# A decoder layer on one core: TensorE's program written out for all heads, the softmax sums in groups 9 and 1, and another order on VectorE and in the transfer queue

## What is computed

```python
def attn(h, Wq, Wk, Wv, Wo, rel_bias):         # 16 heads of 64, S = 2048, two batches
    q, k, v = (proj(W) for W in (Wq, Wk, Wv))   # B,H,S,64
    scores = einsum('bhqd,bhkd->bhqk', q, k) + bias(rel_bias)   # by bucket of the distance
    a = softmax(scores, axis=-1)
    return merge_heads(einsum('bhqk,bhkd->bhqd', a, v)) @ Wo.T
x = x + attn(layernorm(x))
x = x + cross_attn(layernorm(x), ctx)           # 77 keys
x = x + ffn(layernorm(x))                       # a light FFN, and a heavy one for 512 routed rows
```

## Time and profile before

| | us |
|---|---|
| median of 3 runs (lowest, highest) | 3972.28 (3969.41, 3975.57) |
| the profiled execution | 3972.34 |
| its span, from the first to the last instruction | 3970.6 |
| busy in the span: PE, DVE, ACT, POOL | 3727.9, 2466.4, 2004.6, 2681.1 |

### The profile page before, as it was taken

One profiled execution on the slowest core, in us unless ns is written; L12 is line 12 of the kernel. 1 busy time (PEld: TensorE's weight loads), 2 busy tenths in 40 slices (PEclk: granted clock), 3 DMA queues, 4 the chain that ended last, 5 costly groups with the idle time before them and its releaser, 6 DMA issues. The chain is left out here.

```text
span 3970.6 us, 64135 instructions
## 1 busy us (share of the span) xinstructions
PE 3727.9 (94%) x21277; PEld 2216.2 (56%) x21277; DVE 2466.4 (62%) x3356; ACT 2004.6 (50%) x3452; POOL 2681.1 (68%) x1402
## 2 busy tenths in 40 slices
PE   8989999999999989999999999999997999997899
PEld 7754444444444444444444444444446888885377
DVE  3466666666666656666666666666635777775632
ACT  3335555555555555555555555555553555553232
POOL 1128888888888878888988888889893343430010
PEclk9989999999999999999999999999998999998999
DMA  7652222432223452222332222332312333335710
GB/s 221 162 120 63 66 64 71 103 75 69 64 64 81 101 153 64 69 64 67 93 90 66 68 64 67 98 84 65 105 36 88 100 106 103 104 116 174 262 46 22
DMA packets 368370, 366.99 MB, mean 92 GB/s; under 512 B 189339, under 2 KB 261531, under 8 KB 362776
## 3 DMA queue, kind: packets, MB, share of 16 engines
q1 hardware_dynamic: 299064, 336.50, 31.6%
q10 hardware_dynamic: 67168, 20.98, 2.2%
q0 software_dynamic: 1920, 6.29, 0.5%
HBM read 142.64 MB, written 89.70 MB: 59 GB/s over the span
## 5 line engine op out<-in xcount | busy, mean ns | idle before, releaser
L354 POOL TENSOR_TENSOR acc<-acc,probs 128x1024 f32<-128x1024 f32 x894 | 2126.4, 2379 | 306.9 <-ACT probs L814 189.3
L939 DVE TENSOR_REDUCE maxes<-ps 128x2 f32<-128x1024 f32 x1024 | 1253.2, 1225 | 607.6 <-PE ps L610 596.7
L817 ACT ACTIVATE probs<-ps,far_bias 128x1024 f32<-128x1024 f32 (+7 forms) x1280 | 997.4, 819 | 795.4 <-DVE near_s L956 546.0
L641 PE MATMUL ps<-probs,v_head 128*64 128x512 f32 x4096 | 1002.1, 610 | 8.9 <-ACT ctx_out L800 6.9
L629 PE MATMUL ps<-stacks 64*128 64x512 f32 x6144 | 825.7, 398 | 1.8 <-ACT probs L814 1.8
L629 PEld LDWEIGHTS ps<-stacks 64*128 64x128 f32 x6144 | 591.0, 188 | 126.9 <-ACT probs L814 7.9
L610 PE MATMUL ps<-stacks 64*128 64x512 f32 x2048 | 508.0, 494 | 142.4 <-DVE maxes L939 56.9
L610 PEld LDWEIGHTS ps<-stacks 64*128 64x128 f32 x2048 | 194.5, 187 | 700.0 <-DVE maxes L939 464.3
L641 PEld LDWEIGHTS ps<-probs,v_head 128*64 128x64 f32 x4096 | 251.0, 137 | 463.0 <-issue 450.9
L956 DVE TENSOR_TENSOR near_s<-ps,near_bias 128x384 f32<-128x384 f32 (+2 forms) x576 | 265.8, 491 | 58.4 <-PE ps L629 55.3
L962 DVE TENSOR_TENSOR c_q<-ps,c_q 64x512 fp32r<-64x512 f32 x128 | 87.5, 684 | 311.2 <-ACT c_q L773 311.2
(11 more groups left out here) (278 smaller groups left out, 4515.4 us busy)
## 6 DMA issues: line engine op xcount, KB each, us to landing
stacks<-c_q SPq DMA_DIRECT2D x128, 256.0 KB, 4.3
stacks<-c_d SPq DMA_DIRECT2D x64, 512.0 KB, 6.9
stacks<-c_k SPq DMA_DIRECT2D x32, 768.0 KB, 5.5
stacks<-c_k SPq DMA_DIRECT2D x64, 384.0 KB, 7.0
scr_v<-probs ACTq DMA_DIRECT2D x32, 512.0 KB, 4.1
v_head<-scr_v SPq DMA_DIRECT2D x32, 512.0 KB, 8.5
scr_ctx<-ctx_out SPq DMA_DIRECT2D x128, 128.0 KB, 2.3
both_ctx<-scr_ctx SPq DMA_DIRECT2D x32, 512.0 KB, 4.0
```

The lines of the kernel that those rows point to most:

```text
L354: pool.tensor_tensor(acc[:, qb, :], acc[:, qb, :], pr, ALU.add).then_inc(s["summed"], 1)
L641: mm = pe.matmul(ps[64 * half:64 * half + 64, PV, :], v_head[:, side, kt, :], probs[:, st % PT_RING, half * 512:(half + 1) * 512], start=k ...
L817: ins = act.activation(probs[:, st % PT_RING, a:z], sc[:, a:z], ACT.Exp, bias=bias)
L939: dve.tensor_reduce(maxes[:, qt:qt + HALF_GROUPS // 2 + 1:HALF_GROUPS // 2, first_chunk + pair], ps[:, bank:bank + 2, :], AX.X, ALU.max).t ...
```

## The change

TensorE's heads are written out by a Python loop over all heads; the other engines keep their loops. `sum_of` moves from groups 13 and 5 to groups 9 and 1, the reciprocals from 14 and 6 to 10 and 4, and `context` from ahead of steps 31 and 15 to ahead of steps 25 and 13. `project` waits for the sums' copies one quarter earlier, as their groups ask for. On SP `divisors` is cut in two: `spread` issues the four small transfers, `divisors` does the rest. For the second half `spread` stands right behind `fill`; for the first half both stand ahead of the `guard` of the next head. On VectorE the second `largest` of a group stands ahead of `step` and `step_lo`.

```diff
-SUM_GROUPS = {13: 0, 5: 1}
-RECIP_GROUPS = {14: 0, 6: 1}
-CONTEXT_STEPS = {31: 0, 15: 1}
+SUM_GROUPS = {9: 0, 1: 1}
+RECIP_GROUPS = {10: 0, 4: 1}
+CONTEXT_STEPS = {25: 0, 13: 1}
...
-            def divisors(n, qb):
+            def spread(n, qb):
 
                 sp.wait_ge(s["sum_out"], 2 * n + qb + 1)
                 for q in range(QUARTERS):
                     sp.dma_start(part[QP * q:QP * q + QP, :],
                                  sums[QP * q:QP * q + 1, 0:QUARTER].rearrange("o (p c) -> o p c", c=PART)).then_inc(s["spread"], 16)
+
+            def divisors(n, qb):
+
                 sp.wait_ge(s["recip"], 2 * n + qb + 1)
...
                 if nxt:
                     fill(n + 1, 1 - side)
+                if carry:
+                    spread(n - 1, 1)
                 if nxt and not early:
...
                     xn_block(1, reload)
+                if own:
+                    spread(n, 0)
+                    divisors(n, 0)
                 if nxt:
                     guard(n + 1, 1 - side, 0)
...
                 if own:
-                    divisors(n, 0)
                     store_ctx(n, 0)
...
-                    if tb == 1:
+                    if tb == 0:
                         past(pe, s["sum_out"], 2 * (m - 2))
-                    if tb == 3:
+                    if tb == 2:
                         past(pe, s["sum_out"], 2 * (m - 2) + 1)
...
-            heads(pe, head)
+            for n in range(-2, NH):
+                head(n, n // 2, n % 2)
...
+                    if has_max(n, g):
+                        largest(n, side, g, 1)
                     if prep and g in STEP_GROUPS:
                         step(n + 2, STEP_GROUPS[g])
                     if lowered:
                         step_lo(*lowered)
-                    if has_max(n, g):
-                        largest(n, side, g, 1)
```

## The result

| | before | changed |
|---|---|---|
| median, us | 3972.61 (4 runs) | 3796.56 (4 runs, 3794.21 to 3800.00) |
| ratio, 95% interval | 1 | 0.9558 (0.9541 to 0.9574) |
| profiled execution, its span | 3972.34, 3970.6 | 3797.64, 3795.8 |

The kernel became faster by 176 us. The forecast was 3818.6, with 3804 to 3872 as the range. The direction and the mechanism held, but the time lies 22 us under the forecast and 7.4 us under the whole range.

What follows compares the result with a forecast made beforehand. TensorE was taken to set the pace, busy in 95% of 85.07 us a head. Losses of 159.2 us, less 7.3 and 2.6 kept, plus 4.4, gave 153.7 off 3972.3: 3818.6 us, range 3804 to 3872.

Steps and rivals of the forecast that it cites:

- VectorE's order: Groups 11, 12, 15, 0 and 3: maximum first recovers losses of 2.35 us a head, except 0.25 us left.
- floor of a head from the group lengths: Heads 1 to 29: 79.58 us a head if TensorE never waited, added up from undisturbed groups.
- VectorE's residual: Next maximum slightly late in groups with two wide near: 0.25 us a head kept, bounds 0 and 0.7.
- the head of the reload (14): Where normalized rows are reloaded ahead of the fill, the longest wait, 11.8 us, keeps about 2.6 us, once.
- heads 30 and 31: The tail without project, where GpSimd is busy nearly throughout: nothing but 4 us to gain.
- The loop: TensorE's branch: 1.5 us lost in each of 13 pairs of heads, then slow clock; straight code costed at nothing.
- The stacks: Group 3: moving the store lets fill start 7 us earlier, so the wait and slow clock behind it go.
- branch's loss and this wait are one: Group 15's branch and group 3's stacks wait: removing the branch alone lengthens the wait; with slow clock, 3.14 us a head.
- The spread's place: SP's second-half spread behind fill costs nothing; fill ends in group 1, reciprocals over 10 us later.
- The rule that the prediction weighed against the place: Queue transfers go in ring order, so four of 1 KB behind the stacks' would wait for the fill's rest.
- the slower rival: Groups 4 and 10: VectorE waits for spread sums, 4.6 us each, giving 4085; chance 0.09, of which 0.06 slower.
- GpSimd: Last addition fits before the sum in group 9 by 2 to 3 us; as bound, 3867, chance 0.19 with fetch.

Runs made afterwards that it cites:

- D: The change's VectorE part: the group's second maximum ahead of step and step_lo; alone on the kernel before, 3944.86 us.
- e6: The changed kernel with VectorE's old order, step and step_lo ahead of the group's second maximum; 3870.37 us.
- e12: The kernel before with TensorE written out, 102 idle waits a head, and 154 more instructions once ahead, moving the fetch behind the stacks' transfers; 3999.40 us.
- U: The change's TensorE part: heads written out instead of looped; alone on the kernel before, 4003.84 us.
- S: The change's part with the sums' groups, context's steps, project's waits and SP's order; alone on the kernel before, 3892.59 us.
- e5: The changed kernel with TensorE's program left as a loop over two heads; 3827.66 us.
- e11: The kernel before with TensorE written out and 102 idle waits a head, so each head's fetch falls among the stacks' transfers; 4082.58 us.
- e1: The kernel before with TensorE's heads written out and nothing else; 4003.84 us, ratio 1.0090.
- e2: The kernel before with VectorE's other order and nothing else; 3944.86 us, ratio 0.9932.
- e4: The changed kernel with the sums' groups, context's steps and SP's order put back; 3976.55 us, ratio 1.0015.
- e8: The changed kernel with SP's spread and divisors of the first half put back behind the next head's guard; 4082.33 us, ratio 1.0278.
- e7: The changed kernel with SP's spread of the second half put back to where its divisors stand; 3934.57 us, ratio 0.9899.
- e9: The changed kernel with two more weight-sized subtractions on GpSimd in every head from 0 to 29; 3847.50 us, ratio 0.9691.

## Where the prediction held, and the step that failed

The mechanism held, and the sum failed: it had 153.7 us, and 174.8 were measured. The steps that failed are one of its terms and two stretches that it left out. VectorE's order was left 0.25 us a head, 7.3 us, where the heads keep nothing. What stands ahead of head 1 was put at nothing in the sum, and 7.5 us were gained there. What stands behind the heads was put at nothing too, and the profile of the change is 5.8 us shorter there, for a cause that stays open. The range's low end, 3804, had already taken off the 7.3 and 2.6 us and some 5 us "of the heads ahead". So what put the time outside the range is the 5.8 us behind the heads and 3 more ahead of them, less 2 that heads 30 and 31 gained less than forecast.

| step | forecast, us | measured, us |
|---|---|---|
| floor of a head from the group lengths | 79.58 | 79.53 |
| VectorE's residual, 29 heads | 7.3 kept | 0 |
| the head of the reload (14) | 2.6 kept | 0.7 kept |
| a fetch among the stacks' transfers (head 2) | not seen | 0.9 kept |
| heads 1 to 29 together | 149.3 gained | 159.3 |
| ahead of head 0, and head 0 | nothing in the sum | 3.8 and 3.7 gained |
| heads 30 and 31 | 4.4 gained | 2.2 |
| behind the heads | nothing | 5.8 gained |
| the sum, on the span | 153.7 | 174.8 |

**The floor, right.** Group lengths of undisturbed groups, put together in the new order, gave the head to 0.05 us.

**VectorE's order, mechanism right, residual mis-sized.** "I leave 0.25 us a head" is 7.3 of the 21 us. The margin was called nothing, and it is 0.11 us for `step_lo`; but the maximum behind it may start a little late without TensorE noticing, since its pair has 0.3 us in hand at 962.68 and 962.98. A margin of nothing on an engine that isn't the bound was no loss here, and the lower end of the term was the value to take.

**The heads that the sum left out.** I multiplied by 29 heads, but D's places stand in head -1 and head 0 too. e6, which differs from the change by D alone, starts head 0 at 264.8 us and needs 85.1 for it; the change starts it at 260.3 and needs 81.4. The difference lies in head 0's groups 0 and 1 (0.8 and 1.1 us), 3, 12 and 15 (0.5 to 0.6 each). Ahead of head 0 single profiles differ by more than one would like: with the new order it starts at 259.5 to 262.6 us, with the old one at 262.8 to 264.8 (e12 aside), so by the means of the two sorts 2.7 of the 3.8 us are D's.

**Behind the heads: a cause that stays open.** All 14 profiles hold the same work there. Before took 1003.8 us for it, the longest of all; the thirteen others, with U, D or S alone among them, 995.8 to 1001.1. Some 4 of the 5.8 us lie in the third stage. One row of before shows a part: in the third stage a stretch at a clock of 0.68, which the change runs through at 1.00.

```profile
3722.00:3734.00 12.00, 8.23 (x20) 3.47 (x20) 6.02 (x22) 0.00 (x0) 0.00 (x0) 0.68 0.96 344
```

```profile
3551.20:3563.20 12.00, 8.40 (x28) 3.56 (x26) 6.74 (x24) 0.00 (x0) 0.00 (x0) 1.00 1.00 375
```

Why the clock was low there in that execution stays open. The kernel before was profiled once, in an execution at its median, so whether its other executions are as long there is not shown. The lesson is for the range: its low end had some us for the heads ahead, and no allowance for stages that differ by 5 us between profiles.

**The loop, right, with one gap.** The branch's 31 us (e5) are 13 times 1.7 us in group 15, where the text had 1.5, 5 us of slow clock, and 4 us outside these heads. "I cost the straight code at nothing; its cover is that instructions are fetched ahead" holds for TensorE, which never waits for an instruction in the changed heads. It does not hold for the transfers that the fetch meets: 97 us in the heads of e11, against e12. In the changed kernel that price is hidden by the 4 us by which the stacks are early: in heads 5 and 10 the fetch comes about 9 us in and the transfers land at 13.4 and 12.6 in place of 11.6, in heads 4 and 7 at 14.3 and 14.7, in heads 12, 17 and 22, with the fetch 2.3 to 2.6 us in, at 15.1 to 15.3. The last of these is 0.3 us from a loss. Only head 2, with the fetch 4.2 us in, is past the mark: landing at 16.5, wanted at 15.6, 0.9 us lost. *Runtime: NRT & Kernel Launch* of the Trainium skill (section "Instruction fetch mechanics") says that code is fetched in blocks of 256 instructions and 16 KiB while the engine works, and that this is mostly hidden. The rows agree for the engine and for the block (q8 has 16 KB a packet, five heads of 922 instructions repeat after 18 blocks), and the runs add the other side.

**The stacks, right and the largest term.** S takes the store out of the way, `fill` starts 6.3 us earlier, and no run that has S waits longer than about 1 us for `c_k` in any of heads 1 to 29. That U and most of D count only with S was the "branch's loss and this wait are one" of the text; e1, e2 and e4 show it harder than it was put.

**The spread's place, right.** SP's row above has its four transfers issued over 6.64 us, from 10.0 us into head 8; they land at 16.2 to 17.8, the first with the last of the `fill`. Behind nothing but the `guard`, in e8, four such transfers take 3.04 us to issue. It costs nothing, since the reciprocals stand at 24.1. That is 6 us in hand, less than the "over 10" of the prediction, which had the `fill` end in group 1: SP has issued it only in group 2, and it lands at 16.3. The rule that the prediction weighed against the place, on ring order (*DMA: Bandwidth & Descriptors* of the Trainium skill, section "Queues, rings and completion order"), agrees with these rows. The two waits of the slower rival stayed away because of the two places in SP's program, which e7 and e8 price at 138 and 286 us.

**Heads 30 and 31, mis-sized.** I took 4 us (4.4 in the sum); the stretch takes 148.1 in place of 150.3, and waits for exponentials, maxima, stacks and `acc` hold TensorE there as they did.

**GpSimd, right but nearer than it sounded.** The half is complete 2.4 us ahead of the sum in head 8, as the text worked out (2 to 3), and that number suggested slack that isn't there: e9 finds 1.0 us a head.

## What to carry to other kernels

Price an edit in the order in which it would be made: with a wait standing behind it that sets the end, removing a loss in front gives nothing (e4), and the edit that clears the wait collects for all of them. Multiply a loss by every place in which its code stands, the heads of the prologue too, and give the range's favourable end some us for stages that the change doesn't touch. Before moving a transfer in a queue that is run in order, write down which engine waits for it and what that engine holds up meanwhile: four transfers of 1 KB and the `divisors` behind them, a few places apart, decided between -4.4% and +2.8%.

## What the runs showed of the hardware that I had not expected

A block of TensorE's own instructions, 16 KB, which takes 1.0 us on its queue, makes a group of stacks' transfers (some 4 MB) land about 3 us later when it falls among them: 20.5 to 21.2 (one at 19.5) against 17.3 to 18.3 us into the head, in 28 heads each of e11 and e12. The last needed transfer takes most of it: in head 5 of e1 the ninth lands at 18.1 and the tenth at 20.9, in head 4 at 17.3 and 17.8. In the loop of the kernel before the fetch falls at nearly the same places in each pass, some 3.3 and 0.1 us ahead of a head with a branch in front, and 20 to 24 us into each of heads 1 to 28 but 14, and so meets none of the transfers that group 3 waits for. In written-out code it drifts (3.6 blocks a head here), so which heads are hit depends on the count of instructions ahead of them. How a block of 1 us delays others by 3 is not shown: the view of the queues does not tell which of the 16 engines carried it.
